# Token choice and experts in one stage, gathers twelve ahead, ranks summed into one result, closing layer norm in groups of four and three

## The chip, the core and the metric

The kernel runs on one core of a Trainium2 chip. Its engines work from queues of their own and wait for one another by semaphores: TensorE (PE) multiplies matrices into PSUM banks, VectorE (DVE) and ScalarE (ACT) read those banks, GpSimd (POOL) computes and issues the indirect DMAs (gathers of rows by a list of numbers), and SyncE (SP) issues the plain DMAs. The metric is the device time of one execution in microseconds.

## The reference

The input is x, 4 batches of 1024 tokens of width 256. Two layers follow, each an attention and a mixture of experts. The part that the change touches is the end of the second layer: the attention's closing layer norm with gamma and beta, the residual, and then the last mixture, cut here to its core.

```python
# attention of layer 1, its end; x is the residual before it
out = (out - mu) * rsqrt(var + LN_EPS) * gamma + beta          # out = ctx @ wo + bo + layernorm(x)
x = x + out
# mixture of layer 1, on xn = layernorm(x): B = 4, N = 1024, D = 256, E = 8 experts, M = N // E = 128
gate_logits = einsum('bnd,de->bne', xn, gate_w)
gates = sinkhorn(gate_logits)                                   # 8 iterations
vals, idx = top_k(swapaxes(gates, -1, -2), M)                   # each expert takes its 128 best tokens
routed = xn[b_idx, routed_indices]                              # gather of rows
outputs = einsum('ebmd,edf->ebmf', routed, experts) * gate_values
routed_back = zeros_like(xn).at[b_idx, routed_indices].set(outputs)   # a token in several experts keeps one
x = x + routed_back
```

## The kernel before, in words

x stays in on-chip memory as 32 tiles of 128 tokens. The program is a row of stages; `phase` opens each with a barrier, clears its semaphores and sets them (the ISA rows of line 73), four engines taking a quarter each. Inside a stage each engine's instructions stand in the order in which the code writes them; no scheduler moves them. The stages of which the change speaks:

`group_attention`: 512 units of scores. VectorE finds row maxima (L1986), ScalarE takes exponentials (L2029), PE multiplies (L2076, L2089, L2106). Behind the last unit VectorE makes the new x of tiles 0 to 27 in seven groups of four (`new_x`: L1966 scales, L1971 adds the kept x; GpSimd adds beta, L1957; `new_statistics`, L1977, takes the moments). `NEW_AT` says at which steps of the unit count VectorE does so; the steps lie between its waits for PE's context (L1996, L1998) and projection (L2004).

`gated_tiles`: eight groups of four tiles. VectorE normalises (`normalise`, L2204, tile gt_xn, two buffers), SP stores the rows for the gathers (routed_rows, L2192), PE turns them (L2279), ScalarE copies (L2243), PE makes the gate products (L2287), ScalarE copies (L2250), PE turns (L2295), ScalarE keeps the logits (L2254). The last four tiles get their closing norm here (`last_tiles`), and then ScalarE's second square root (L152) stands ahead of its copy of the second group.

`sinkhorn`: a chain between PE and VectorE, untouched.

`top_tokens`: PE turns the gates (L2412), VectorE takes for the 32 pairs of batch and expert their 128 best tokens, 8 at a time (L2432 to L2435), PE turns the list, VectorE writes m_index (L2442). Then 32 masks (L2446, one per pair, "which token is this", two buffers), each multiplied by PE in eight products of one column (L2421), and from the ranks the place of each token (L2449 to L2460).

`routed_experts`: SP loads the expert weights (L2488). GpSimd gathers the rows of pair n (L2509, four buffers, held until PE has turned pair n-4), PE turns (L2533), ScalarE copies (L2569), PE multiplies (L2544), VectorE scales by the gate (L2582, tile re_y, four buffers), SP stores (L2495, routed_outputs). Then GpSimd gathers for each of the 32 tiles its rows (L2519, re_got, four buffers, from the batch's results once all are stored), VectorE adds them to x (L2587), and SP stores the output (L2499), in a loop with a register count. All 64 gathers stand in one queue, and all 64 stores of results and output in another.

Of the kernel before, what the change touches and what calls it, by code (L numbers as in the profile page):

```python
# [1802 lines left out]
def group_attention(nc, g, parts, values, x_kept, qs, ks, v, gamma, beta, gw, gate):  # L1803
# [54 lines left out]
    with phase(nc) as (e, semaphore, begin):  # L1858
# [14 lines left out]
        NEW_AT = [UNITS + k for k in (3, 7, 14, 18, 22, 26, 30, 34)]  # L1873
# [291 lines left out]
def gated_tiles(nc, g, qs, gamma, beta, gw, logits, rows_out):  # L2165
# [4 lines left out]
    STEPS, TH = T // C, C // HALVES  # L2170
    with phase(nc) as (e, semaphore, begin):
        sb = lambda n, shape, dt=F32: e.enter_context(nc.sbuf_tensor(f"gt_{n}", shape, dt))
        sem = lambda n: semaphore(f"gt_{n}")
        xn = [sb(f"xn{u}", [P, C, D]) for u in range(2)]
# [6 lines left out]
        rows_kept = [sem(f"rows_kept{u}") for u in range(2)]  # L2181
# [5 lines left out]
        @block.sync  # L2187
        def _(sp):
            rows = rows_out.rearrange("(i c p) d -> i p c d", c=C, p=P)
            for i in range(STEPS):  # L2190
                sp.wait_ge(xn_ready, ONE + C * (i + 1))
                sp.dma_start(rows[i], xn[i % 2][:]).then_inc(rows_kept[i % 2], 16)  # L2192
            for u in range(2):
                sp.wait_ge(rows_kept[u], ONE + 16 * (STEPS // 2))

        @block.vector
        def _(dve):
            def normalise(i):
                if i >= 2:
                    dve.wait_ge(xnT_done, ONE + HALVES * (i - 1))  # L2200
                    dve.wait_ge(rows_kept[i % 2], ONE + 16 * (i // 2))
                for c in range(C):
                    t = C * i + c
                    nc.vector.tensor_scalar(xn[i % 2][:, c, :], g.x[:, t, :], g.mean[:, t:t + 1], g.rstd[:, t:t + 1],  # L2204
                                            ALU.subtract, ALU.mult).then_inc(xn_ready, 1)

            def last_tiles():
                tiles = range(READY, T)
                for t in tiles:
                    nc.vector.scalar_tensor_tensor(g.x[:, t, :], g.x[:, t, :], g.mean[:, t:t + 1], gamma[:],  # L2210
                                                   ALU.subtract, ALU.mult).then_inc(scaled_ready, 1)
                dve.wait_ge(scaled_ready, ONE + LATE_TILES)
                for t in tiles:
                    nc.vector.scalar_tensor_tensor(g.x[:, t, :], g.x[:, t, :], g.rstd[:, t:t + 1], kept_tiles(qs, t, 1)[:, 0],
                                                   ALU.mult, ALU.add).then_inc(x_ready, 1)
                dve.wait_ge(x_ready, ONE + LATE_TILES)
                nc.vector.tensor_tensor(g.x[:, READY:T, :], g.x[:, READY:T, :], beta[:].unsqueeze(1).broadcast_to([P, LATE_TILES, D]),
                                        ALU.add).then_inc(beta_ready, 1)
                dve.wait_ge(beta_ready, ONE + 1)
                for t in tiles:  # L2220
                    nc.vector.bn_stats(g.stats[:, t, :], g.x[:, t, :]).then_inc(stats_ready, 1)
                dve.wait_ge(stats_ready, ONE + LATE_TILES)
# [6 lines left out]
            last_tiles()  # L2229
            closing.moments(dve, 1, READY)  # L2230
            closing.inverses(dve, 1, READY)
            for i in range(2, STEPS):
# [407 lines left out]
```

## Time and profile before

| what | us |
|---|---|
| median of 3 runs (2344.79 to 2349.75) | 2348.84 |
| the profiled execution, its own time | 2363.76 |
| its span, first to last instruction | 2362.0 |
| attention's last stage ends, about | 2080 |
| first instruction of top tokens | 2152.7 |
| first gather of the experts | 2238.9 |

TensorE is busy 2011.9 us of the span (85%), VectorE 1704.1 (72%), ScalarE 1213.4 (51%), GpSimd 474.0 (20%). These are averages over stages with different limits: most of the span is attention and the first mixture, which the change does not touch. A row of the timeline gives the start, the duration, the engine, the line, the operation, what it writes and reads, how often, and in brackets how long the engine was idle before and what released it. "issue" means that it waited for nothing that the profile shows.

### The profile page before, as it was taken

The page shows a single profiled execution, that of the slowest core. Times are in us where ns is not written, and L with a number is a line of the kernel's source. Part 1 is how long each engine was busy: PE and PEld are TensorE (multiplying, and loading weights), DVE is VectorE, ACT ScalarE, POOL GpSimd, SP SyncE. Part 2 cuts the span into 40 slices and gives each one's busy share as a digit, 9 for nine tenths or more (in the row PEclk, how much of TensorE's full clock was granted, in tenths as well). Part 3 has the DMA queues.
Part 4 walks back from the last instruction along what each step waited for, and adds up shares of the span by engine and source line. Part 5 has one row for each costly group of instructions (what it writes and reads, how often), then busy time and mean ns, then how long its engine had stood idle before and what let it go on. Part 6 is the DMA issues. An engine that isn't in the chain of part 4 may idle for free. (4 is left out here: it accounts for less than half of the span.)

```text
span 2362.0 us, 49456 instructions
## 1 busy us (share of the span) xinstructions
PE 2011.9 (85%) x18325; PEld 1356.7 (57%) x18325; DVE 1704.1 (72%) x2695; ACT 1213.4 (51%) x2196; POOL 474.0 (20%) x610
## 2 busy tenths in 40 slices
PE   5889888799979999989978899999999999971270
PEld 4667666468879999978867333343343343330150
DVE  5666666566658888856644789999999999647822
ACT  4455454343256666632233278888888888530010
POOL 1010001010022322224343112112212211300054
PEclk9899999799989999999989589999999999675585
DMA  2000000191043333333268886854864701020054
GB/s 90 2 0 0 0 0 0 60 342 62 28 157 124 120 111 120 107 100 113 89 206 281 105 73 59 73 38 43 67 41 44 62 20 37 19 72 0 27 159 136
DMA packets 222809, 188.18 MB, mean 80 GB/s; under 512 B 121533, under 2 KB 201369, under 8 KB 220505
## 3 DMA queue, kind: packets, MB, share of 16 engines
q1 hardware_dynamic: 202872, 146.71, 30.9%
q0 software_dynamic: 18080, 27.17, 4.3%
q10 hardware_dynamic: 1728, 12.58, 1.5%
q8 instruction: 81, 1.33, 0.3%
q14 instruction: 48, 0.39, 0.1%
HBM read 121.37 MB, written 64.75 MB: 79 GB/s over the span
## 5 line engine op out<-in xcount | busy, mean ns | idle before, releaser
L2029 ACT ACTIVATE ga_probT<-banks 128x512 f32<-128x512 f32 x1024 | 556.7, 597 | 172.7 <-PE banks L2089 124.7
L1986 DVE TENSOR_REDUCE ga_nmax<-banks 128x1 fp32r<-128x1024 f32 x512 | 610.4, 1218 | 27.9 <-PE banks L2076 26.7
L2076 PE MATMUL banks<-a_ks,a_qs 48*128 48x512 f32 x1024 | 390.8, 465 | 9.5 <-PEq L77 5.7
L2089 PE MATMUL banks<-a_qs,a_ks 49*128 49x512 f32 x1024 | 390.1, 461 | 2.3 <-ACT ga_probT L2029 2.3
L2106 PE MATMUL banks<-ga_probT,a_v 128*32 128x256 f32 x4096 | 342.1, 408 | 6.2 <-ACT ga_o L2035 6.2
L2076 PEld LDWEIGHTS banks<-a_ks,a_qs 48*128 48x128 f32 x1024 | 158.9, 195 | 224.7 <-DVE ga_nmax L1986 171.5
L1952 POOL DMA_DIRECT2D a_qs<-ga_max_rows x256 | 130.8, 519 | 578.4 <-DVE ga_max_rows L1993 537.1
L1447 PE MATMUL banks<-rb_xT,rb_own_w 128*128 128x256 f32 x1872 | 232.1, 283 | 5.2 <-DVE rb_xT L1313 3.5
L1447 PEld LDWEIGHTS banks<-rb_xT,rb_own_w 128*128 128x128 f32 x1872 | 224.5, 190 | 11.5 <-issue 8.1
L2106 PEld LDWEIGHTS banks<-ga_probT,a_v 128*32 128x32 f32 x4096 | 82.9, 110 | 203.8 <-ACT ga_probT L2029 146.8
L1153 PE MATMUL banks<-m_xnT,sh_w 128*128 128x512 f32 x768 | 184.2, 398 | 6.6 <-DVE sh_w L942 5.3
L1289 POOL DMA_INDIRECT rb_xb<-normalised_rows,m_source x78 | 101.9, 1307 | 391.3 <-PE banks L1436 229.1
L2089 PEld LDWEIGHTS banks<-a_qs,a_ks 49*128 49x128 f32 x1024 | 158.1, 193 | 20.0 <-ACT ga_probT L2029 16.8
L1153 PEld LDWEIGHTS banks<-m_xnT,sh_w 128*128 128x128 f32 x768 | 145.9, 192 | 39.4 <-issue 9.5
L370 DVE TENSOR_REDUCE wa_nmax<-banks 128x4 f32<-128x512 f32 x128 | 87.0, 680 | 96.1 <-PE banks L584 96.1
L449 ACT ACTIVATE wa_probT<-banks 128x512 f32<-128x512 f32 x128 | 76.4, 597 | 136.3 <-PE banks L596 136.3
L1305 DVE TENSOR_TENSOR rb_own_w<-m_w,rb_own_w 128x1024 fp32r<-128x1024 f32 x78 | 95.2, 1221 | 68.7 <-ACT rb_own_w L1378 64.7
L1468 PE MATMUL banks<-rb_own_w,rb_glu 128*128 128x256 f32 x936 | 119.0, 283 | 3.4 <-DVE rb_own_w L1309 3.4
L1468 PEld LDWEIGHTS banks<-rb_own_w,rb_glu 128*128 128x128 f32 x936 | 112.1, 189 | 3.6 <-DVE rb_own_w L1309 3.6
L596 PE MATMUL banks<-ident,wa_prob 128*128 128x128 f32 x512 | 88.6, 298 | 23.5 <-ACT wa_prob L442 23.5
L442 ACT ACTIVATE wa_prob<-wa_ex 128x512 f32<-128x512 f32 x128 | 80.5, 629 | 52.2 <-DVE wa_ex L372 51.5
L278 POOL TENSOR_TENSOR wa_q_heads<-wa_q,wa_head_rows 128x512 f32<-128x512 f32 x32 | 32.6, 1039 | 365.9 <-ACT wa_q L483 365.9
(327 smaller groups left out, 3240.3 us busy)
## 6 DMA issues: line engine op xcount, KB each, us to landing
rb_w_f<-in_L_ffn_rw_dram SPq DMA_DIRECT2D x39, 512.0 KB
m_xnT<-xnT_parts ACTq DMA_DIRECT2D x12, 1024.0 KB, 4.8
sorted_out<-rb_yb SPq DMA_DIRECT2D x39, 256.0 KB, 2.1
m_w<-in_L_ffn_rw_dram SPq DMA_DIRECT2D x2, 4096.0 KB, 20.3
values<-pg_v SPq DMA_DIRECT2D x16, 512.0 KB, 3.1
a_v<-values SPq DMA_DIRECT2D x16, 512.0 KB, 8.8
a_qs<-queries_rounded SPq DMA_DIRECT2D x28, 256.0 KB, 8.6
a_ks<-keys_rounded SPq DMA_DIRECT2D x28, 256.0 KB, 10.4
```

Of the source, the lines that this page charges most:

```text
L596: last = nc.tensor.transpose(b_pt[k][:, P * j:P * (j + 1)], prob[k][:, j, :], g.ident[:])
L1153: last = nc.tensor.matmul(bank[m % 2][:], w[a][:, k, P * m:P * (m + 1)], xnT[s][:, b, k, :], start=(k == 0 and a + b == 0), stop=(k == KD ...
L1289: nc.gpsimd.indirect_dma_start(out=xb[j % 2][:, h, :], out_offset=None, in_=rows, in_offset=bass.IndirectOffsetOnAxis(ap=source[:, 2 * j + ...
L1305: nc.vector.tensor_tensor(flat(own_w[1]), of(w, n), flat(own_w[0]).bitcast(F32), ALU.subtract).then_inc(ready, 1)
L1447: last = nc.tensor.matmul(bank[h][:, R * m:R * (m + 1)], w[a][:, k, at:at + P], xT[b][:, k, :], start=(k == 0 and a + b == 0), stop=(k == ...
L1468: last = nc.tensor.matmul(b_y[:, D * r:D * (r + 1)], glu[a][:, m, P * r:P * (r + 1)], own_w3[b][:, m, :], start=(m == 0 and a + b == 0), s ...
L1952: nc.gpsimd.dma_start(dst, src).then_inc(max_in[1][b % 2], 16)
L1986: nc.vector.tensor_reduce(nmax[b % 2][:, at:at + 1], slot[:], axis=AX.X, op=ALU.max, negate=True).then_inc(use_read, 1)
L2029: nc.scalar.activation(probT[k % SETS][2 * h + n][:], b_t[ring_place["weights", w] % RING][:], ACT.Exp, scale=SCALE).then_inc(exp_ready, 1)
L2076: return nc.tensor.matmul(slot[:, HALF * kh:HALF * (kh + 1)], qs[a][rows, n, P * q:P * (q + 1)], ks[a][rows, n, HALF * kh:HALF * (kh + 1)] ...
L2089: nc.tensor.matmul(bank[:], ks[a][rows, 2 * gp + n, P * kt:P * (kt + 1)], qs[a][rows, 2 * gp + n, HALF * hf:HALF * (hf + 1)], start=True, ...
L2106: last = nc.tensor.matmul(b_o[at:at + BL, cols], v[c % SLOTS][:, h, 2 * gp + n, kt, :], probT[k % SETS][2 * h + n][:, cols], start=(kt == ...
```

## The change

It has three parts. First, `top_tokens` and `routed_experts` become one stage. The gathers start when the index is written; GpSimd may be twelve pairs ahead (`AHEAD`), with a buffer for each of the 32 pairs and of the 32 results; the masks stand between the scalings on VectorE, two beside each expert; the places are worked out at pair 16; the additions to x begin at pair 26. Second, each mask is multiplied by a matrix that is zero but for one column, so that all pairs add into one 32x1024 result, which is copied and turned once. Third, the closing layer norm: `NEW_AT` puts four groups ahead of VectorE's wait for the projection and three behind, and in `gated_tiles` three buffers let three more groups be normalised between the steps of the last four tiles.

```diff
-        NEW_AT = [UNITS + k for k in (3, 7, 14, 18, 22, 26, 30, 34)]
+        NEW_AT = [UNITS + k for k in (3, 4, 5, 6, 14, 15, 16, 17)]
...
-    STEPS, TH = T // C, C // HALVES
+    STEPS, TH, KEPT = T // C, C // HALVES, 3
...
             normalise(0)
             normalise(1)
-            last_tiles()
+            late_scaled()
+            late_sums()
+            normalise(2)
+            late_betas()
+            late_statistics()
+            normalise(3)
+            dve.wait_ge(stats_ready, ONE + LATE_TILES)
             closing.moments(dve, 1, READY)
+            normalise(4)
             closing.inverses(dve, 1, READY)
-            for i in range(2, STEPS):
+            for i in range(5, STEPS):
                 normalise(i)
...
+            pool.wait_ge(index_ready, ONE + 1)
+            for n in range(BE):
+                if n >= AHEAD:
+                    pool.wait_ge(t_done, ONE + n - AHEAD + 1)
+                if n >= SL:
+                    pool.wait_ge(taken_in[n % SL], 16 * (n // SL))
+                nc.gpsimd.indirect_dma_start(out=taken[n][:], out_offset=None, in_=rows,
+                                             in_offset=bass.IndirectOffsetOnAxis(ap=index[:, n:n + 1], axis=0)
+                                             ).then_inc(taken_in[n % SL], 16)
+            pool.wait_ge(zero_kept, ONE + 16 * B)
+            for t in range(T):
+                if t % TB == 0:
+                    for s in range(SL):
+                        pool.wait_ge(kept[s], ONE + 16 * (t // TB + 1) * (E // SL))
+                if t == 0:
+                    pool.wait_ge(place_ready, ONE + 1)
+                if t >= SL:
+                    pool.wait_ge(got_in[t % SL], 16 * (t // SL))
...
+            def ranks(n):
+                pe.wait_ge(is_ready, ONE + n + 1)
+                for h in range(2):
+                    cols = slice(S // 2 * h, S // 2 * (h + 1))
+                    last = nc.tensor.matmul(b_r[0:BE, cols], rank_col[:, BE - 1 - n:2 * BE - 1 - n], is_token[n % HOTS][:, cols],
+                                            start=(n == 0), stop=(n == BE - 1))
+                last.then_inc(rank_done, 1)
...
+            transposes(0)
             for n in range(BE):
+                if n + 1 < BE:
+                    transposes(n + 1)
+                products(n)
+                for m in range(LEAD + 2 * n, min(LEAD + 2 * n + 2, BE)):
+                    ranks(m)
+                if n == PLACES_AT:
+                    ranks_T()
...
+            for n in range(LEAD):
+                hot(n)
             for n in range(BE):
+                for m in range(LEAD + 2 * n, min(LEAD + 2 * n + 2, BE)):
+                    hot(m)
+                weighed(n)
+                if n == PLACES_AT - 1:
+                    dve.wait_ge(rank_done, ONE + BE)
+                    nc.vector.tensor_copy(ranks_s[:], b_r[0:BE, :]).then_inc(ranks_copied, 1)
+                if n == PLACES_AT:
+                    places()
+                if n >= ADDS_AT:
+                    added(n - ADDS_AT)
+            for t in range(BE - ADDS_AT, T):
+                added(t)
+
+
+LEAD, PLACES_AT, ADDS_AT, AHEAD = 2, 16, 26, 12
```

`transposes`, `products`, `weighed` and `added` are the steps of before, unrolled instead of looped by batch; `weighed` still has four buffers and waits for the store of pair n-4. SP's list is unchanged: the weights, the 32 stores of results, then the loop of 32 output stores.

On PE, where the masks and the experts meet (tt_ and re_ are the stages' prefixes; re_taken the gathered rows, re_w the weights, re_takenT the turned rows), the program before has:

```order
L2415 MATMUL banks<-ident,tt_top 128x32
L2416 MATMUL banks<-ident,tt_top_at_f 128x32
L2421 MATMUL banks<-tt_rank,tt_is_token 128x1 x256
L64 UNCONDITIONAL_BRANCH
L2523 UNCONDITIONAL_BRANCH
L2533 MATMUL banks<-ident,re_taken 128x128 x2
```

and the changed one, from the same two turns on:

```order
L2517 MATMUL banks<-ident,re_top 128x32
L2518 MATMUL banks<-ident,re_top_at_f 128x32
L2485 MATMUL banks<-re_is_token,re_rank_col 32x512 x4
L2501 MATMUL banks<-ident,re_taken 128x128 x4
L2509 MATMUL banks<-re_w,re_takenT 128x256 x2
```

The 256 one-column products ahead of the stage's end are gone; four products of 512 columns now stand behind each of the first 15 experts, and the next expert's turns stand between.

On VectorE in the gated tiles, around the last four tiles' norm, the difference is this (gt_xn is the normalised group, a_beta the added vector):

```order
 L142 RECIPROCAL rstd<-gt_std 128x32
 L2204 TENSOR_SCALAR gt_xn<-x,mean,rstd 128x256 x8
-L2210 SCALAR_TENSOR_TENSOR x<-x,mean,a_gamma 128x256 x4
-L2214 SCALAR_TENSOR_TENSOR x<-x,rstd,a_qs 128x256 x4
-L2217 TENSOR_TENSOR x<-x,a_beta 128x1024
-L2221 BN_STATS stats<-x 128x6 x4
+L2211 SCALAR_TENSOR_TENSOR x<-x,mean,a_gamma 128x256 x4
+L2217 SCALAR_TENSOR_TENSOR x<-x,rstd,a_qs 128x256 x4
+L2204 TENSOR_SCALAR gt_xn<-x,mean,rstd 128x256 x4
+L2222 TENSOR_TENSOR x<-x,a_beta 128x1024
+L2228 BN_STATS stats<-x 128x6 x4
+L2204 TENSOR_SCALAR gt_xn<-x,mean,rstd 128x256 x4
```

Eight normalisations now stand ahead of the second set of moments (L128 and following, behind this piece), which stood directly behind L2221.

## Rows read from the trace of the kernel before

**Rows 1.** Busy time by stretch: engine sums with instruction counts, clock, DMA share, GB/s.
```profile
2320.00:2340.00 20.00, 0.00 (x0) 0.00 (x0) 6.81 (x16) 0.00 (x0) 13.89 (x15) 0.50 0.42 124
```

**Rows 2.** Timeline of VectorE at the end of top tokens.
```profile
2217.63 0.19 DVE L2442 TENSOR_TENSOR m_index<-tt_indexT,tt_batch_row 128x32 uint32<-128x32 f32 x1
2217.74 15.27 DVE L2446 TENSOR_SCALAR tt_is_token<-tt_token,tt_indexT 128x1024 bf16<-128x1024 f16 x32
...
2236.35 0.18 DVE L2460 TENSOR_SCALAR m_place<-tt_row 128x32 uint32<-128x32 f32 x1
```

**Rows 3.** Timeline of GpSimd: first gather, first after the hole, last.
```profile
2238.93 1.04 POOL L2509 DMA_INDIRECT re_taken<-routed_rows,m_index  x1 [0.44 <-issue]
...
2303.44 0.94 POOL L2519 DMA_INDIRECT re_got<-routed_outputs,m_place  x1 [8.81 <-DVE x L2587]
...
2337.21 0.94 POOL L2519 DMA_INDIRECT re_got<-routed_outputs,m_place  x1 [0.30 <-DVE x L2587]
```

**Rows 4.** Tile re_taken: what ended engines' idle time, us and times.
```profile
  PE banks L2533: 13.9, 10
```

**Rows 5.** Timeline of SP: output stores, all, two single ones, the last 21.
```profile
2303.49 56.72 SPq L2499 DMA_DIRECT2D out_dram<-x  x32
...
2314.13 0.00 SPq L2499 DMA_DIRECT2D out_dram<-x  x1
...
2333.12 0.71 SPq L2499 DMA_DIRECT2D out_dram<-x  x1
...
2341.55 18.66 SPq L2499 DMA_DIRECT2D out_dram<-x  x21
```

**Rows 6.** DMA queues in 2324 to 2330: packets, MB, share. The only queue.
```profile
q0 software_dynamic: 240, 0.66, 37.0%
```

**Rows 7.** Timeline of PE in the experts; stretch 2254 to 2256, columns as rows 1.
```profile
2248.40 2.07 PE L2544 MATMUL banks<-re_w,re_takenT 128*128 128x256 f32 x4
...
2268.24 1.03 PE L2544 MATMUL banks<-re_w,re_takenT 128*128 128x256 f32 x4
2269.10 0.38 PE L2533 MATMUL banks<-ident,re_taken 128*128 128x128 f32 x2
...
2254.00:2256.00 2.00, 2.00 (x13) 1.74 (x12) 0.97 (x2) 0.77 (x2) 1.26 (x3) 1.00 0.60 187
```

**Rows 8.** Gated tiles: timeline of VectorE, ScalarE, PE; stretch 2100 to 2102.
```profile
2093.82 2.68 DVE L2204 TENSOR_SCALAR gt_xn<-x,mean,rstd 128x256 f32<-128x256 f32 x8
...
2093.20 0.30 ACT L152 ACTIVATE gt_std<-gt_var,gt_eps 128x4 f32<-128x4 f32 x1 [6.57 <-DVE gt_var L136]
2093.41 1.06 ACT L2243 ACTIVATE gt_xnT<-banks 128x512 f32<-128x512 f32 x2
...
2096.25 3.58 PE L2287 MATMUL banks<-gt_xnT,a_gw 128*8 128x512 f32 x4
...
2101.18 1.88 PE L2287 MATMUL banks<-gt_xnT,a_gw 128*8 128x512 f32 x4
...
2100.00:2102.00 2.00, 2.00 (x14) 1.17 (x14) 0.71 (x3) 1.62 (x4) 0.00 (x0) 1.00 0.68 234
```

**Rows 9.** Timeline around the entry into top tokens.
```profile
2151.00 0.42 DVE L2368 TENSOR_TENSOR m_gates<-sk_p,sk_expert_sum 128x256 f32<-128x256 f32 x1
2152.66 1.41 PEld L2412 LDWEIGHTS banks<-ident,m_gates 128*32 128x32 f32 x8 [4.56 <-issue]
```

**Rows 10.** Attention's end: timeline of VectorE; stretch 2040 to 2060.
```profile
2040.66 0.69 DVE L2004 TENSOR_TENSOR x<-banks,x 128x512 f32<-128x512 f32 x1 [11.93 <-PE banks L2134]
...
2042.05 1.66 DVE L1966 SCALAR_TENSOR_TENSOR x<-x,mean,a_gamma 128x256 f32<-128x256 f32 x4
...
2046.72 2.67 DVE L1966 SCALAR_TENSOR_TENSOR x<-x,mean,a_gamma 128x256 f32<-128x256 f32 x4
...
2052.40 2.68 DVE L1966 SCALAR_TENSOR_TENSOR x<-x,mean,a_gamma 128x256 f32<-128x256 f32 x4
...
2040.00:2060.00 20.00, 20.00 (x93) 6.30 (x91) 19.00 (x42) 10.37 (x19) 7.08 (x3) 0.50 0.00 1
```

More of the change, by code:

```diff
@@ L2369, in _, with routed_experts @@
                                         ALU.mult).then_inc(p_ready, 1)
-def top_tokens(nc, g, gates, index, value, place):
+def routed_experts(nc, g, gates, rows, outputs, out):
     E = gates.shape[3]
@@ new lines, in routed_experts @@
+        takenT = [sb(f"takenT{s}", [P, KD, M]) for s in range(SL)]
+        y = [sb(f"y{s}", [M, D]) for s in range(SL)]
+        got = [sb(f"got{t}", [P, D]) for t in range(T)]
+        zero = sb("zero", [1, D])
+        consts, gT_done, step, top_ready, topT_done, index_ready = [sem(n) for n in (
+            "consts", "gT_done", "step", "top_ready", "topT_done", "index_ready")]
+        is_ready, rank_done, place_ready = sem("is_ready"), sem("rank_done"), sem("place_ready")
+        ranks_copied, ranksT_done = sem("ranks_copied"), sem("ranksT_done")
@@ new lines, in transposes, with products @@
+            def transposes(n):
+                s = n % SL
+                pe.wait_ge(taken_in[s], 16 * (n // SL + 1))
+                if n >= TS:
+                    pe.wait_ge(t_ready, ONE + n - TS + 1)
+                for k in range(KD):
+                    last = nc.tensor.transpose(b_t[n % TS][:, M * k:M * (k + 1)], taken[n][:, P * k:P * (k + 1)], g.ident[:])
+                last.then_inc(t_done, 1)
+            def products(n):
+                pe.wait_ge(t_ready, ONE + n + 1)
+                if n >= YS:
+                    pe.wait_ge(y_ready, ONE + n - YS + 1)
+                for k in range(KD):
+                    last = nc.tensor.matmul(b_y[n % YS][:, 0:D], takenT[n % SL][:, k, :], w[:, n % E, k, :],
+                                            start=(k == 0), stop=(k == KD - 1))
+                last.then_inc(y_done, 1)
@@ L2597, in mixture1 @@
         gates = sb("gates", [P, TB, B, E])
-        index, value, place = sb("index", [M, BE], U32), sb("value", [M, BE]), sb("place", [P, T], U32)
         sinkhorn(nc, g, logits, gates)
-        top_tokens(nc, g, gates, index, value, place)
-        routed_experts(nc, g, rows, outputs, index, value, place, out)
+        routed_experts(nc, g, gates, rows, outputs, out)
 def program(nc, g, out):
```

277 lines of the change are left out of this document (108 added, 169 removed).

## The prediction

> **What bounds the kernel now.** I read the table by stretches first. Attention ends near 2080 us, gated tiles near 2119, Sinkhorn near 2151; then come top tokens to 2236.5 and routed experts to 2362.0. In the last two stages no compute engine is full: from 2320 to 2340 PE does nothing, VectorE works 6.8 us of 20, and even GpSimd, the busiest, 13.9 [rows 1]. So the end is set by a chain, not by a busy engine, and I followed it backwards in three timelines.
>
> VectorE has the experts' token numbers (m_index) at 2217.82 us. Then it makes 32 masks in 15.3 us and the places, done at 2236.53 [rows 2]. None of that is needed by the first gather, which yet starts at 2238.93 because it lies in the next stage [rows 3]. From there GpSimd issues 64 gathers, one each 1.25 us (0.95 busy, 0.30 between) when nothing holds it, the last ending at 2338.15: 99.2 us for a chain worth 64 x 1.25 = 80. The missing 19 us are holes: 13.9 us in ten waits for transposes that free one of four buffers, and one of 8.8 us [rows 3, 4] (3.3 of these 22.7 are the ordinary spacing).
>
> Last comes a tail of 23.85 us behind the last gather. In it SP issues 21 of the 32 output stores, 0.89 us each (18.66/21) [rows 5]. They are late though their rows were ready: while GpSimd gathers without a pause, SP's stores come ever farther apart: eight in the first 10.6 us (2303.49 to 2314.13), then four gaps of 6.9 us on average up to 2341.55, the last 8.4 [rows 5]. The queue view agrees: from 2324 to 2330 the queue that carries the stores moved nothing, while gathers filled 37% of the DMA engines [rows 6].
>
> **The change part by part.** The sum is made on the profiled execution (span 2362.0, own time 2363.76), then carried to the median 2348.84 by subtraction. The profiled one stands 0.6% above the median, which I carry over as it is.
>
> (a) *Start of the gathers.* They now wait for the index in the same stage: 2238.93 - 2217.82 = 21.1; with 0.1 for the wait, **-21.0**. The masks and places go beside the experts.
>
> (b) *The chain of 64 gathers.* Twelve ahead instead of four, and every result buffer separate. Ideal 79.9 (64 x 1.248) against 99.2: -19.3. What is late next: gather n needs the transposes of expert n-12, and PE now does two rank sums, four products in all, beside each of the first 15 experts. An expert costs 1.09 us at 2.4 GHz (2268.24 to 2269.10 the products, and 0.22 for the transposes), 2.5 at 1.2 GHz (2.07 + twice 0.22) [rows 7]. The new 32x512 product in bf16 has no row. From below it is the 256-column f32 pass, 0.26 us (1.03/4); from above the 512-column f32 pass, 0.47 (1.88/4) [rows 7, 8]. I take 0.26, since the operands are half as wide. So an expert with four such products is 1.09 + 1.04 = 2.13 at the high clock. I let PE begin at 2222, 4 us behind the first gather's issue, and I let it work 7 us at the low clock, as now from 2247 to 2254, when the granted clock is 1.00 [rows 7]: expert 15 at 2229 + 13.3 x 2.13 = 2257, the transposes of 19 at about 2262. Gather 31 would be ready to issue at 2218 + 31 x 1.25 = 2257. So **5 us** of stall come back (with 0.47 per product: 2229 + 13.3 x 2.97 + 4.4 = 2273, 16 us; with no price for the clock or products: 0). VectorE (two masks and one scaling, 3 x 0.48 = 1.4 us per expert) and the ring of four y buffers lie below 2.1. The copy of the ranks and the places (3.5 us now, from the masks' end at 2233.0 to 2236.53 [rows 2]; I count 5 for both) delay it at experts 15 and 16, covered by y banks three deep and gathers twelve ahead. Term: -19.3 + 5 = **-14.3**, ends -19 and 0.
>
> (c) *The tail.* Now one y store plus 11 output stores got out beside 28 gathers in 35 us. In the new order SP must first issue the last 12 to 15 y stores beside the 32 result gathers (40 us), and by the same rate that uses up what SP gets. So 29 to 32 output stores are left instead of 21: 8 x 0.89 = **+7**. From below: if SP keeps pace, 2 are left and the tail is 5, so -19; from above all 32 are left, +10. I take +7, by the rows in which SP and GpSimd work together.
>
> At this place the Trainium skill, "DMA: Bandwidth & Descriptors", section "Queues, rings and completion order", says otherwise: each DMA engine takes turns between its queues packet by packet. By it the stores would get their turns and the tail would be the lower end. The trace disagrees from 2314 on, with 6.9 us between stores, so the row decides and the rule is only a rival.
>
> (d) *Gated tiles.* On VectorE, eight normalisations (tiles 2 and 3 of four, 2.68 us) now stand ahead of the late moments [rows 8]. But ScalarE's square root still stands ahead of its second copy: now it waits 6.57 us for the moments and copies at 2093.41. It will copy at 2096.2. PE does the third transposes early, then stands idle until 2097.3, where now its gate products begin at 2096.25 [rows 8]: +1.05. PE has the low clock in them now (3.58 us for four, against 1.88 at the next step, when the granted clock is 1.00) [rows 8]; after a longer idle the rise moves from 2100 to some 2103, and 3 us of work at half speed cost up to 1.5 more. The steps behind are PE's own, 3.17 us each, so nothing gives it back. **+2.2**, ends 0 and +3.
>
> (e) *Stage entries.* One stage is gone (in (a)). The new one sets six semaphores per engine instead of two. The entry with two takes 1.24 us (2151.42 to 2152.66), that with three to four 1.66 (2236.53 to 2238.19) [rows 2, 9]; 0.28 each gives **+0.8** (0 to +1.2).
>
> (f) *Closing layer norm inside attention.* Four groups before VectorE's wait for the projection, three behind. A group takes 5.69 us; two more fit from 2028.7 to 2040.1, in an idle of 11.93 us that ends at 2040.66 [rows 10]. But PE is the bound there, 20.00 us busy in 20.00 at clock 0.50, and asks VectorE for nothing until the projection. **0** (if the groups overran by 3 us, 30 us of slack lie behind).
>
> (g) Ranks summed into one 32x1024 result, and turned: 256 small products leave, 64 and eight turns come. All of it is in (b).
>
> Sum: -21.0 - 14.3 + 7 + 2.2 + 0.8 = **-25.3**. 2363.76 - 25.3 = 2338.5 in the profiled state, 2348.84 - 25.3 = **2323.5** at the median.
>
> **The rivals.**
> 1. *SP keeps pace.* y stores now come beside gathers each 1.5 us without a queue; the starvation appears only after 10 us without a hole. With holes from PE the stores flow, output stores start near 2276 and follow the sums. Tail 5 instead of 31: -51, time 2298. Against it: the result gathers have no more holes than now.
> 2. *The port.* A mask is 0.477 us (15.27/32) for 1024 elements and now runs while GpSimd issues. In the rows an addition group of VectorE stretches from 1.67 to 2.67 us where GpSimd computes [rows 10]. If each mask holds up one gather for its length, 32 x 0.48 = 15.3 us enter the chain, less 5 already idle: +10, time 2334. The Trainium skill, "SBUF — State Buffer", section "Who interferes with whom", has this as a lock: VectorE's two-port modes block GpSimd wholly, descriptor writing included. No row of the present kernel has masks beside gathers.
> 3. *SP and GpSimd exclude each other.* 64 gathers x 1.25 plus 64 stores x 0.89 = 137 us from 2218, plus 2 at the end: 2357; with (d), (e) 2360, time 2347: no change.
> 4. *Slower: the y ring.* y stores pass four buffers. If, with GpSimd now never resting, each y store takes the 6.9 us that output stores take between 2314 and 2341, then 32 x 6.9 = 221 us stand in place of 44, and PE, then gathers, wait on it: 2218 + 221 + 31 + 3 = 2473, time 2460. The forecast has 32 experts in 44 us, 1.4 each, so it decides from 1.4 + 25.3/32 = 2.2 us per y store. For it: the spacing in [rows 5]. Against it: gathers stop when twelve ahead, and holes let stores through.
> 5. *Products nearly as dear as f32.* The upper end of (b), +11: 2334.
>
> **How the numbers follow.** Forecast and its own range (2310 to 2332): 0.48. Rival 1: 0.20. Rivals 2 and 5: 0.18. Rival 3: 0.06. Rival 4: 0.03, and milder forms of it that end between forecast and no change: 0.05. Within 0.2% (4.7 us, about what a measurement here can tell from no change) lies half of rival 3: 0.03. Slower: rival 4 and what rival 3 might overrun, 0.04. Faster: 0.93. Range 2297 to 2340: it takes rival 1 at its edge and leaves out rivals 3 and 4.
>
> **What would show it.** (a) First re_taken gather 0.1 to 0.3 us behind re_index. (b) 64 gathers within 80 to 88 us, holes only where transposes are late, between the 22nd and 32nd; the 32x512 products at 0.26 us when the clock is high. (c) From the last gather's end some 31 us with 29 or more output stores in it, and gaps of about 7 us between stores while GpSimd is full. (d) The second gt_xnT copy at about 3 us later after the stage's start. (f) PE as busy as now until the stage ends. The forecast falls if output stores follow the sums (rival 1), if a gather beside a mask takes over 1.3 us (rival 2), or if the scalings wait for their buffer most of the time (rival 4).

## The result, and the profile after

The changed kernel takes 2330.12 us (median of six runs, 2322.77 to 2333.79), the kernel before 2349.3 beside it. The ratio is 0.9912, with a 95% interval of 0.9887 to 0.9937: 19 us less, where 25 were forecast. Two later comparisons with the kernel unchanged gave 0.9958 (0.9925 to 0.9991) and 0.9916 (0.9886 to 0.9946). The time lies inside the range. But two of the large terms are wrong, and their errors partly cancel: it is inside by luck.

The two profiled executions differ by 41 us (spans 2362.0 and 2321.0), more than the medians. Most of the surplus lies ahead of the change's main part. The experts' token numbers (re_index, formerly m_index) are ready 22.6 us earlier, and that moment varies much between profiles of the same code: 2217.6 and 2202.2 us in two of the kernel before, 2195.1, 2195.8 and 2209.1 in three of the kernel after. So I compare from the start of that instruction to the span's end, "index to end" below: 144.4 and 141.0 us before, 125.9, 129.7 and 127.7 after. That is 15 us less on the means.

First the steps that came as forecast. VectorE's timeline at the index, then GpSimd's with the first gather right behind it (the answer to [rows 2, 3]):

```profile
2195.07 0.19 DVE L2560 TENSOR_TENSOR re_index<-re_indexT,re_batch_row 128x32 uint32<-128x32 f32 x1
```
```profile
2195.55 1.04 POOL L2463 DMA_INDIRECT re_taken<-routed_rows,re_index  x1 [63.75 <-DVE re_index L2560]
```

The wait is gone: 0.3 us from the index's end to the gather instead of 21.1. PE's timeline then shows the new rank products, which had no row before, beside an expert's own work (transposes, products):

```profile
2206.93 1.04 PE L2485 MATMUL banks<-re_is_token,re_rank_col 128*32 128x512 bf16 x4
2207.90 0.44 PE L2501 MATMUL banks<-ident,re_taken 128*128 128x128 f32 x2
2208.18 1.03 PE L2509 MATMUL banks<-re_w,re_takenT 128*128 128x256 f32 x4
```

Four 32x512 products take 1.04 us, 0.26 each, the lower end of the price, as chosen. From 2219.5 to 2244 an expert comes every 2.20 us (forecast 2.13), with PE busy 24.09 us of 24.50.

Now what came otherwise. Busy time by stretch (columns as in [rows 1]):

```profile
2196.00:2206.00 10.00, 8.65 (x29) 3.98 (x28) 3.40 (x9) 1.15 (x3) 7.57 (x9) 0.65 0.37 105
2206.00:2219.50 13.50, 8.18 (x32) 3.59 (x30) 2.79 (x7) 0.79 (x3) 8.65 (x9) 0.77 0.43 127
2219.50:2244.00 24.50, 24.09 (x101) 12.49 (x102) 13.32 (x31) 4.09 (x12) 10.39 (x11) 0.92 0.37 111
2251.00:2257.00 6.00, 6.00 (x34) 5.16 (x34) 2.36 (x6) 1.77 (x5) 4.72 (x5) 1.00 0.77 226
2257.00:2280.00 23.00, 6.88 (x22) 4.45 (x20) 2.60 (x6) 1.15 (x3) 17.24 (x19) 0.59 0.47 133
2280.00:2292.00 12.00, 5.99 (x14) 4.16 (x14) 5.46 (x16) 1.04 (x3) 0.79 (x2) 0.64 0.24 77
2292.00:2306.00 14.00, 0.00 (x0) 0.00 (x0) 6.21 (x18) 0.00 (x0) 11.53 (x8) 0.50 0.68 200
```

Between 2257 and 2280 PE, VectorE and ScalarE are all nearly idle (6.88, 2.60 and 1.15 us of 23), and GpSimd issues 19 gathers, about the most it can. Experts 26 to 31, which need 1.09 us each, take 34 us. This is ScalarE's timeline there, the copy of one expert's turned rows; "remote" is a wait whose end comes so late that the profile matches it to no instruction or transfer:

```profile
2255.40 0.38 ACT L2540 ACTIVATE re_takenT<-banks 128x256 f32<-128x256 f32 x1 [0.70 <-issue]
2258.85 0.38 ACT L2540 ACTIVATE re_takenT<-banks 128x256 f32<-128x256 f32 x1 [3.07 <-PE banks L2501]
2263.13 0.38 ACT L2540 ACTIVATE re_takenT<-banks 128x256 f32<-128x256 f32 x1 [3.90 <-remote]
2268.78 0.38 ACT L2540 ACTIVATE re_takenT<-banks 128x256 f32<-128x256 f32 x1 [5.26 <-remote]
2282.06 0.38 ACT L2540 ACTIVATE re_takenT<-banks 128x256 f32<-128x256 f32 x1 [12.90 <-remote]
```

The copy at 2282.06 belongs to the thirtieth expert and waits for PE alone, for that expert's two transposes. PE's timeline has them here:

```profile
2265.44 0.64 PE L2501 MATMUL banks<-ident,re_taken 128*128 128x128 f32 x2
```

They end at 2266.07, 16.0 us before the copy starts. The trace also records when PE's update of the semaphore took effect: 2282.04, and ScalarE starts 0.02 us later. So it is the producer's signal that is late, not the waiting engine. VectorE's scaling in the same stretch shows 9.69 us "remote". The experts' late rows then reach GpSimd:

```profile
2279.79 0.95 POOL L2475 DMA_INDIRECT re_got<-routed_outputs,re_place  x1 [0.30 <-issue]
2291.95 4.62 POOL L2475 DMA_INDIRECT re_got<-routed_outputs,re_place  x1 [11.21 <-DMA routed_outputs<-re_y]
2296.87 0.94 POOL L2475 DMA_INDIRECT re_got<-routed_outputs,re_place  x1 [0.30 <-issue]
```

A second standstill of this kind lies early, under the first gathers. The chain of waits from the index to the end, its five longest pieces:

```profile
2211.05 8.40 another core or an unknown queue
2258.87 4.24 another core or an unknown queue
2263.16 5.60 another core or an unknown queue
2268.80 13.24 another core or an unknown queue
2291.95 4.62 POOL re_got L2475
```

So the chain from the first gather to the end of the last became longer, 110.1 us instead of 99.2 (forecast 84.9). The tail behind it became shorter, 15.3 instead of 23.85 (forecast 31): GpSimd's hole of 11.2 us let the last y stores and two output stores out. In contrast to [rows 5], SP's timeline has all 32 output stores at 0.91 us apiece, 15 of them behind the last gather:

```profile
2290.14 29.12 SPq L2443 DMA_DIRECT2D out_dram<-x  x32
```

### The profile page after: what moved, and what is told of

Same layout as the page of the kernel before. It is cut to its first block and busy times, and to the rows that moved or that the text cites. A ratio compares the mean times of both kernels' runs of the same rounds, so it can differ in the third digit from the quotient of the medians.

```text
span 2321.0 us, 48875 instructions
## 1 busy us (share of the span) xinstructions
PE 1999.7 (86%) x18141; PEld 1345.6 (58%) x18141; DVE 1701.1 (73%) x2696; ACT 1214.0 (52%) x2196; POOL 480.5 (21%) x612
## 5 line engine op out<-in xcount | busy, mean ns | idle before, releaser
L2089 PE MATMUL banks<-a_qs,a_ks 49*128 49x512 f32 x1024 | 379.7, 451 | 2.3 <-ACT ga_probT L2029 2.3
L2106 PE MATMUL banks<-ga_probT,a_v 128*32 128x256 f32 x4096 | 331.0, 396 | 6.4 <-ACT ga_o L2035 6.4
L1447 PEld LDWEIGHTS banks<-rb_xT,rb_own_w 128*128 128x128 f32 x1872 | 224.7, 190 | 10.9 <-issue 7.6
L2089 PEld LDWEIGHTS banks<-a_qs,a_ks 49*128 49x128 f32 x1024 | 153.8, 188 | 15.5 <-ACT ga_probT L2029 12.4
```

The source lines that it names most:

```text
L1447: last = nc.tensor.matmul(bank[h][:, R * m:R * (m + 1)], w[a][:, k, at:at + P], xT[b][:, k, :], start=(k == 0 and a + b == 0), stop=(k == ...
L2089: nc.tensor.matmul(bank[:], ks[a][rows, 2 * gp + n, P * kt:P * (kt + 1)], qs[a][rows, 2 * gp + n, HALF * hf:HALF * (hf + 1)], start=True, ...
L2106: last = nc.tensor.matmul(b_o[at:at + BL, cols], v[c % SLOTS][:, h, 2 * gp + n, kt, :], probT[k % SETS][2 * h + n][:, cols], start=(kt == ...
```

## The experiments

The runs fell on three chips: e1 to e4 on the first, e5 to e8 on the second, e9 to e12 on the third. Which one gave the result above is not on record.

Two theories fit this profile, and two more had to be asked. Theory 1: while GpSimd issues indirect gathers one right behind another, the other engines' waits for each other end late. Theory 2: straight-line code is fetched late (the two loops over batches are unrolled now). Theory 3: the ring of four y buffers. Theory 4: PE's pace. Against theory 2 the trace already says that the instruction queues moved nothing between 2246 and 2310.

**Only the closing layer norm and the gated tiles, on the kernel before.**

```diff
-        NEW_AT = [UNITS + k for k in (3, 7, 14, 18, 22, 26, 30, 34)]
+        NEW_AT = [UNITS + k for k in (3, 4, 5, 6, 14, 15, 16, 17)]
 ... (gated_tiles as in the kernel after, top_tokens and routed_experts as before)
```

> Only the part on the closing layer norm and on the gated tiles (NEW_AT, the third xn buffer, the later tiles' work in pieces between the tiles) on the kernel before; choice of tokens and experts stay as they were. In the two profiled executions the last attention tiles (2000 to 2060 us) ran at a granted clock of 0.50 to 0.54 before and 0.71 to 0.82 after, and the index was ready 22 us earlier. If that is the work of this part: about 2330 us (ratio 0.99), and the granted clock of 2000 to 2060 is above 0.7 here too. If it is chance of the execution: 2350 to 2353 us (ratio 1.000 to 1.002), with +0.7 us from the gated tiles, and then the whole gain of 19 us comes from the merged stage.

Ratio 0.997 (0.9935 to 1.0005), index to end 142.0 us, the granted clock was 1.00 in 2000 to 2020 and 0.59 in 2020 to 2040. The clock there follows the execution, not the code: in the same two stretches a second profile of the kernel before had 0.74 and 0.83, one of the kernel after 1.00 and 0.60. Whether this part gives nothing or up to 15 us isn't settled by so wide an interval. The rest of the gain is put down to the merged stage.

**Experts' gathers four ahead.**

```diff
-LEAD, PLACES_AT, ADDS_AT, AHEAD = 2, 16, 26, 12
+LEAD, PLACES_AT, ADDS_AT, AHEAD = 2, 16, 26, 4
```

> The kernel after with the experts' gathers four ahead instead of twelve. Theory 1 (a run of indirect gathers that GpSimd issues one right behind another holds up the other engines' waits, on ScalarE and VectorE above all): GpSimd pauses from the fifth gather on, the 8.4 us of standstill at 2211 to 2219.5 go or shrink to 2 us, the first result gather starts 6 to 8 us earlier, and the time is 2321 to 2325 us (after: 2330); the standstills under the result gathers stay. Theory 2 (straight-line code that is fetched late) and theory 3 (the ring of four y buffers): the standstill stays where it is, 2329 to 2332 us. Theory 4 (PE's pace, twelve ahead is needed to feed it): every gather's landing, 2.7 us, now shows in part, 2335 us or more.

0.9903 (0.9875 to 0.9931), index to end 128.8 us: no faster than after, so as a time my expectation missed. But the profile says more. The 8.4 us standstill is gone, also the one among experts 26 to 31 nearly (last y store issued at 2267.4 instead of 2289.4), and the 32 result gathers have no hole: GpSimd's group of them is

```profile
L2475 POOL DMA_INDIRECT re_got<-routed_outputs,re_place x32 | 30.4, 950 | 9.7 <-issue 9.7
```

in 39.8 us, 2258.3 to 2298.1. The chain is then 98.4 us, 11.7 less than after, and all of it comes back in the tail: five output stores got out beside the gathers, at distances up to 8.4 us, and 27 were left, 30.0 us of tail against 15.3.

```profile
2281.25 0.70 SPq L2443 DMA_DIRECT2D out_dram<-x  x1
...
2289.65 0.70 SPq L2443 DMA_DIRECT2D out_dram<-x  x1
...
2298.05 0.70 SPq L2443 DMA_DIRECT2D out_dram<-x  x1
...
2303.64 22.74 SPq L2443 DMA_DIRECT2D out_dram<-x  x27
```

**Result gathers behind the last expert.**

```diff
-                        pool.wait_ge(kept[s], ONE + 16 * (t // TB + 1) * (E // SL))
+                        pool.wait_ge(kept[s], ONE + 16 * B * (E // SL))
-LEAD, PLACES_AT, ADDS_AT, AHEAD = 2, 16, 26, 12
+LEAD, PLACES_AT, ADDS_AT, AHEAD = 2, 16, 32, 12
```

> The kernel after with the result gathers held back until all 32 experts' rows are kept, and the additions behind the last expert. Theory 1: with no gather beside them experts 23 to 31 run at 1.09 us each as experts 17 to 22 did, the last y store is issued at about 2262 and the 32 gathers run from about 2264 to 2304; behind them some 20 output stores of 0.88 us are left, so the end is at about 2323 of the span (now 2321), 2330 to 2334 us. Theories 2 and 3: the last nine experts take 34 us as now (2255 to 2289) and the gathers end at 2330, 2350 us or more.

0.994 (0.9905 to 0.9974), 2343 us; index to end 137.8. Theory 1's mechanism is borne out: without gathers beside them the last eleven copies of ScalarE come 1.08 to 1.29 us apart and nothing is "remote".

```profile
2262.35 0.38 ACT L2540 ACTIVATE re_takenT<-banks 128x256 f32<-128x256 f32 x1 [0.70 <-PE banks L2501]
...
2273.40 0.38 ACT L2540 ACTIVATE re_takenT<-banks 128x256 f32<-128x256 f32 x1 [0.70 <-PE banks L2501]
```

The time missed by 10 us. The early standstill was longer here (two y stores were 9.95 us apart), so the gathers began at 2278, 74.6 us behind the index instead of 69, and the tail was 23.2 us instead of 19.

**Eight y buffers.**

```diff
-    y = [sb(f"y{s}", [M, D]) for s in range(SL)]        # and kept likewise
+    y = [sb(f"y{s}", [M, D]) for s in range(8)]
```

> The kernel after with eight y buffers and eight kept semaphores instead of four. Theory 3 (the experts stand still since a y buffer is not stored yet): the holes before the multiplications by value go, experts end at 2262 instead of 2289, the hole of 11.2 us in the result gathers goes, 2316 to 2320 us. Theories 1 and 2: nothing is moved by it, 2329 to 2332 us, holes on VectorE and ScalarE at the same places.

0.9928 (0.9894 to 0.9962), index to end 129.0: theory 3 falls. ScalarE's timeline has the same row of standstills:

```profile
2266.21 0.38 ACT L2540 ACTIVATE re_takenT<-banks 128x256 f32<-128x256 f32 x1 [4.59 <-remote]
2271.89 0.38 ACT L2540 ACTIVATE re_takenT<-banks 128x256 f32<-128x256 f32 x1 [5.29 <-remote]
2284.53 0.38 ACT L2540 ACTIVATE re_takenT<-banks 128x256 f32<-128x256 f32 x1 [12.26 <-remote]
```

**A pause at every fourth, and at every eighth result gather** (both with four ahead).

```diff
+                if t and t % 4 == 0:          # 8 in e6_pause8 and e11_pause8_again
+                    pool.wait_ge(got_in[(t - 1) % SL], 16 * ((t - 1) // SL + 1))
```

> The kernel after with the experts' gathers four ahead (as in e2_ahead4) and a pause in the result gathers: every fourth waits until the one before it has landed, some 1.7 us. In e2_ahead4's profile the 32 result gathers ran without a gap (2258.3 to 2298.1), SP issued only 5 of 32 output stores beside them, at distances of 5.7 to 8.4 us, and the 27 others behind them, 27.9 us. Theory 1 (a run of back-to-back gathers holds up engines that wait for another engine): the stores flow at 0.9 to 1.5 us in and after each pause, the gathers take 40 + 7 x 1.7 = 52 us, 3 to 6 stores are left, 5 us: index to end 59 + 52 + 6 = 117 us (e2: 128.8, after: 125.9), the time 2319 to 2323. If the stores lag for another reason (the DMA engines' turns, as the prediction had it): they stay behind, 40 + 12 + 25, 2340 us.

> As e5_pause4 with the pause at every eighth result gather. Theory 1: within each run of eight (10 us) the distance of the stores grows to 5 or 7 us, and a pause of 1.7 us lets 1 or 2 through; gathers 40 + 3 x 1.7 = 45 us, some 18 stores left, 18 us: index to end 59 + 45 + 18 = 122 us, the time 2324 to 2328. If what counts is the number of pauses and not the length of a run, 24 stores are left and 2331.

Index to end is 121.1 us with seven pauses and 111.8 with three. A pause adds 2.5 to 3.4 us, where I had counted 1.7. In both the stores follow the gathers: two and three are left behind the last, where I had expected 18 with the pause at every eighth. These two profiles can't say that the pauses did it, since on this chip long runs held nobody up either (below). In the profiles of the two other chips the start of the hold-up can be dated: the first step that takes over 4.5 us begins 10.5 to 11.4 us after the run of gathers did (kernel after: 2195.55 and 2206.17, 2196.26 and 2206.71, 2209.60 and 2220.82; eight y buffers: 2199.51 and 2210.14; results last: 2204.07 and 2215.50; before: 2303.44 and 2314.13, [rows 5]; in its second profile after 13.5). That is eight or nine gathers in. It holds for runs behind a quiet stretch. Where other gathers had ended only 1.3 to 1.4 us earlier, such a step came sooner: 6.5 us into the run of eight in the kernel before (2284.93 and 2291.41), 5.1 us in e1_norm_alone (2274.68 and 2279.75), 7.3 us in e11_pause8_again (2254.69 and 2261.97).

The times of these two were odd, though. On that chip the kernel before took 2326 us, and the ratios were 1.001 (0.9972 to 1.0048) and 0.9967 (0.9949 to 0.9984), with 2319 to 2323 and 2324 to 2328 us expected against a kernel before of 2357.

**Plain loads in place of the result gathers.**

```diff
-                nc.gpsimd.indirect_dma_start(out=got[t][:], out_offset=None, in_=outputs[t // TB], ...
+                nc.gpsimd.dma_start(got[t][:], outputs[t // TB][P * (t % TB):P * (t % TB + 1), :]) ...
```

> As e2_ahead4 with the 32 result gathers replaced by plain loads of 128 rows in their order on GpSimd's queue (the rows are not put back in their tokens' places, so the output differs). It asks what in a run holds the others up. If it is the making of 128 descriptors from indices: the plain loads are issued faster or slower, and SP's stores flow beside them at 0.9 to 1.5 us each, with fewer than 8 stores left behind them. If it is the traffic of GpSimd's queue as such: the same distances of 5 to 8 us and over 20 stores left.

Index to end 93.4 us, five stores left. But the loads came mostly in twos to fours with waits of 0.8 to 1.8 us between, so there never was a long run, and the chip is the one where long runs of gathers held nobody up: it doesn't tell indices from traffic.

**The same pause in the kernel before.**

> The kernel before with the pause of e5_pause4 in its result gathers and nothing else. In its profile 21 of 32 output stores were left behind the last gather, 21.7 us, and the stores beside the gathers came at distances of 3.6 to 8.4 us. Theory 1: the gathers take 12 us more (part of it in the wait of 9.8 us that is there), the stores left shrink from 21 to 3 to 6: -15 to -17 us; the sum is -5 to -3 us, 0.998 of before. The other cause (the DMA engines' turns): +12 us, 1.005.

Index to end 130.7 us, 10 to 14 less than in both profiles of the kernel before, and three stores left instead of 21 and 19, as theory 1 has it. Yet the time was 1.0083 (1.0036 to 1.0129) of the kernel before on this chip, the wrong way. The profile says why the comparison misleads. Up to the fourth result gather its code is the kernel before's, and there, with 28 gathers from 2250.76 to 2284.72 and never over 0.51 us between two, ScalarE's copies are never more than 2.4 us apart and keep their pace to the end of the run:

```profile
2250.76 0.94 POOL L2509 DMA_INDIRECT re_taken<-routed_rows,m_index  x1 [0.51 <-PE banks L2535]
...
2284.72 0.95 POOL L2521 DMA_INDIRECT re_got<-routed_outputs,m_place  x1 [0.30 <-issue]
```
```profile
2281.41 0.38 ACT L2571 ACTIVATE re_takenT<-banks 128x256 f32<-128x256 f32 x1 [0.70 <-PE banks L2535]
2282.59 0.38 ACT L2571 ACTIVATE re_takenT<-banks 128x256 f32<-128x256 f32 x1 [0.79 <-PE banks L2535]
2283.67 0.38 ACT L2571 ACTIVATE re_takenT<-banks 128x256 f32<-128x256 f32 x1 [0.70 <-PE banks L2535]
```

So no hold-up is there for a pause to take away. Two runs of the kernels unchanged followed:

> The kernel before, unchanged, for a second profile. The runs e5 to e8 were on another chip than e1 to e4: there the kernel before took 2326 us instead of 2357, a pause in its result gathers made it 17 us slower instead of faster, and in e6_pause8's profile SP's output stores came at 1.2 us beside runs of eight gathers, where e2_ahead4's profile on the first chip had 5.7 to 8.4 us. Theory 1a (runs of back-to-back gathers hold the other engines up on some chips or in some executions only): each profile shows the one or the other. Where the hold-up is missing, output stores follow the gathers at 1.25 us, 2 to 4 are left behind the last gather instead of 21, and index to end is 118 to 124 us; where it is there, 142 to 146 as in the two profiles so far. Theory 1b (the hold-up comes from the profiler's own traffic and the chips differ in something else): this profile has it on any chip.

> The kernel after, unchanged, on the same chip as e9_before_again. Without the hold-up the merged stage does what its order allows: first result gather 53 us behind the index (now 56), 32 gathers in 40 us, end 3 us later: index to end 95 to 100 us, 20 to 25 us less than the kernel before there, ratio 0.989 to 0.991. With the hold-up: 124 to 127 us against 142 to 146, ratio 0.991 to 0.992.

They fell on the third chip (before 2353.5 us there). The hold-up was in both: output stores 5.65, 7.70 and 7.72 us apart and 19 left in the one, in the other copies of ScalarE 8.1, 9.9 and 11.3 us apart; index to end 141.0 and 129.7, ratio 0.9958 (0.9925 to 0.9991). Last, the pause and the kernel after side by side:

> e6_pause8 unchanged, beside the kernels before and after on one chip. In eight profiles the standstills begin some 10 to 11 us after the start of a run of back-to-back gathers (8 or 9 gathers in), and grow to 8.4 us a step; runs of at most eight stay under that. If that is the rule on this chip too: the stores come at 1.2 us beside the gathers, at most 4 are left behind the last one, index to end 110 to 114 us against 125 to 130 (after) and 141 to 145 (before): 0.985 to 0.988 of before and 0.994 of after. If it goes as on the chip of e5 to e8, where the times were 0.997 of before: 0.995 to 1.000 of before, and the profile of after (e12_after_third) should then show no standstill, with an index to end of 95 to 100 us.

> The kernel after, unchanged, on the same chip as e11_pause8_again. With the standstills (as in two profiles so far): the first at 10 to 11 us behind the first gather, experts' end and the result gathers' hole of 11 to 15 us, index to end 125 to 130 us, 0.991 to 0.996 of before. Without them: 95 to 100 us, 0.98 to 0.99 of before, and faster than e11_pause8_again by about 9 us, the price of its three pauses.

The pause at every eighth gave 0.9856 (0.9804 to 0.9907) of the kernel before, the kernel after 0.9916 beside it: 2319.3 against 2335.5 us. So this version beats both kernels on this chip. It differs from the kernel after by four ahead too, which alone changed nothing that could be measured on the first chip. Index to end is 114.1 against 127.7, with six stores left against 16. GpSimd's timeline shows one run of eight and the pause behind it, and SP's shows twelve stores around that run, eight of them beside it, 1.2 us apart where the run without pauses had 8.4:

```profile
2286.72 0.95 POOL L2477 DMA_INDIRECT re_got<-routed_outputs,re_place  x1 [3.40 <-DMA re_got<-routed_outputs,re_place]
...
2295.48 0.94 POOL L2477 DMA_INDIRECT re_got<-routed_outputs,re_place  x1 [0.30 <-issue]
2299.70 0.94 POOL L2477 DMA_INDIRECT re_got<-routed_outputs,re_place  x1 [3.27 <-DMA re_got<-routed_outputs,re_place]
```
```profile
2285.04 13.65 SPq L2443 DMA_DIRECT2D out_dram<-x  x12
```

One gap of 8.5 us is left in it, between y stores: right ahead of the first eight result gathers stand five of the experts' without a hole, a run of thirteen from 2254.69. ScalarE stands still in it:

```profile
2258.45 0.39 ACT L2542 ACTIVATE re_takenT<-banks 128x256 f32<-128x256 f32 x1 [0.70 <-issue]
2261.97 0.38 ACT L2542 ACTIVATE re_takenT<-banks 128x256 f32<-128x256 f32 x1 [3.14 <-PE banks L2503]
2266.97 0.39 ACT L2542 ACTIVATE re_takenT<-banks 128x256 f32<-128x256 f32 x1 [4.62 <-remote]
2273.33 0.38 ACT L2542 ACTIVATE re_takenT<-banks 128x256 f32<-128x256 f32 x1 [5.97 <-remote]
```

The same code on the second chip, in e6_pause8, did not stand still there, though its run was longer: eighteen gathers from 2238.15 to 2259.59 (GpSimd's timeline), and 13 to 15 us into it ScalarE keeps its pace:

```profile
2238.15 1.10 POOL L2463 DMA_INDIRECT re_taken<-routed_rows,re_index  x1 [1.41 <-PE banks L2503]
...
2259.59 0.95 POOL L2477 DMA_INDIRECT re_got<-routed_outputs,re_place  x1 [0.30 <-issue]
```
```profile
2251.07 0.38 ACT L2542 ACTIVATE re_takenT<-banks 128x256 f32<-128x256 f32 x1 [0.70 <-PE banks L2503]
2252.16 0.38 ACT L2542 ACTIVATE re_takenT<-banks 128x256 f32<-128x256 f32 x1 [0.70 <-PE banks L2503]
2253.43 0.38 ACT L2542 ACTIVATE re_takenT<-banks 128x256 f32<-128x256 f32 x1 [0.89 <-PE banks L2503]
```

## Why the prediction was right or wrong

**(a) Start of the gathers: right.** Forecast -21.0, measured -20.8: 0.3 us behind the index where 21.1 stood.

**(b) The chain: wrong in sign.** Forecast -14.3, measured +10.9. PE's part was right: 2.20 us for an expert with ranks, 0.26 for a product. The early standstill taken off, the 31 gathers behind the first take 53.7 - 8.4 = 45 us, where the forecast had 44. The step that failed is the list of what comes late next. I named PE, VectorE and the y ring, each with its work, and none of them is late through its work. I had seen that gathers without a hole keep SP's stores back [rows 5], and priced it for SP alone. In these profiles it holds for what waits on PE as well, and filling the holes with gathers twelve ahead makes the long runs that set it off: with four ahead the early standstill went, with the result gathers held back the late one. In the kernel before the experts' gathers waited ten times for a free buffer [rows 4], and I booked these waits as 13.9 us lost; between them only the last run, of eight, held a step up, by 5.0 us (ScalarE, 2291.4 to 2296.4). That those holes let the other engines run fits these profiles. On the second chip the same code ran nearly without them, and nobody stood still.

**(c) The tail: right as a mechanism, wrong in its case.** Forecast +7, measured -8.5. The forecast supposed result gathers without a hole. Four ahead makes just that case, and there the tail is 30.0 us with 27 stores, against 31 and 29. In the kernel after the standstill of the experts opened a hole of 11.2 us. The prediction set the spacing of the stores against the rule of turns between queues in the Trainium skill, "DMA: Bandwidth & Descriptors", section "Queues, rings and completion order". That reading does not hold: already SP's issues are that far apart. One turn of SP's loop is six instructions in the trace, the store and five of register work and branching, which the timeline leaves out. In the kernel before they take 0.03 to 0.37 us each around 2304. From 2325 to 2341 nearly all take 0.70 us or more, most of them 0.70 apart, though only one of the six waits for another engine. In e2_ahead4 it is the same from 2281 on, and twelve such steps are the 8.4 us. A store's first packet comes 4.4 to 7.0 us behind its issue there, and what holds it back until then isn't shown; all its packets are then done within 1.0 us beside the gathers. So these runs neither refute the rule nor bear it out.

(b) and (c) together: forecast -7.3, measured +2.4. The time came inside the range because the error of (b), 25.2 us, was met by one of (c), 15.5 us the other way; nothing in the prediction foresaw that.

**(d), (e): right within 1.5 us.** The gated tiles take 39.14 us instead of 38.45, +0.7 (forecast +2.2). The moments are waited for 8.91 us instead of 6.57, and PE's gate products begin later, as foretold, at the same 3.58 us; the clock's rise was not put off:

```profile
2071.63 0.30 ACT L152 ACTIVATE gt_std<-gt_var,gt_eps 128x4 f32<-128x4 f32 x1 [8.91 <-DVE gt_var L136]
```
```profile
2072.95 3.58 PE L2300 MATMUL banks<-gt_xnT,a_gw 128*8 128x512 f32 x4 [5.54 <-ACT gt_xnT L2256]
```

The entry into the merged stage takes 1.99 us instead of 1.24, +0.75 (forecast +0.8; four more semaphores at the prediction's own 0.28 each would have made 1.1).

**(f): open.** Forecast 0; the run of this part with (d) alone gave -7 us, with an interval from -15 to +1.

**The sum.** (a) to (c) take away 18.4 us in the two profiles and 15 on the means of all that were taken, and (d) and (e) give back 1.4 ahead of the index; the medians say 19.2, 11.6 and 18.8 less. Forecast 25.3.

**The rivals.** Rival 1 (SP keeps pace where there are holes) is true of the mechanism and happened in part: the tail came by a hole. Its time needed holes without their cost. Rival 2, the port: the masks ran beside gathers only at a few places. Here two of them cover one gather, which takes 0.97 us:

```profile
2208.56 0.88 DVE L2565 TENSOR_SCALAR re_is_token<-re_token,re_indexT 128x1024 bf16<-128x1024 f16 x2
```
```profile
2208.58 0.97 POOL L2463 DMA_INDIRECT re_taken<-routed_rows,re_index  x1 [0.30 <-issue]
```

The same is seen at 2213.6 (0.97) and, for most of a gather, at 2219.7 (0.94); the longest gather that touches a mask took 1.16. A lock for the length of a mask would add up to 0.48 for each one. The Trainium skill, "SBUF — State Buffer", section "Who interferes with whom", states such a lock; these rows do not show it. Rival 3 fails by the eight stores beside one run of eight gathers, 9.7 us in all, where one after the other they would need 17. Rival 4, the y ring: y stores were up to 10.5 us apart, as it said, but eight buffers changed nothing. The rows are made late, not stored late. Rival 5: the product is 0.26.

**What stays open.** First, why a run of gathers holds the others up. It strikes PE's signals, for which ScalarE and VectorE wait (recorded up to 16.0 us after PE's work ended in the kernel after, up to 18.2 in its second profile), and SP's own instructions; VectorE's waits for landed gathers end on time (additions every 1.25 us in the kernel before from 2304 to 2338).

Theory 1b, that recording the execution takes part in it, was not tested, and the record speaks for it in one form. Each gather's landing counts as 16 updates in the kernel's waits, so 64 gathers should leave 1024 records of them in the trace. The profiles of e5, e6 and e7 have all 1024, that of e8 1023, and in none of the four does a long run of gathers hold anyone up. All the others miss more than half (the kernel before has 250, the kernel after 395, e11_pause8_again 463), and all of them have the hold-up. SP's register instructions that take 0.70 us while waiting for nobody fit this as well. Every timed execution on record was recorded in this way, so no run tells what an unrecorded one does. As stated in the expectation, that recording causes it on any chip, the theory is wrong.

Second, what is different on the second chip. If the part ahead of the index took there what it took in any profile (2194 to 2229 us), the kernel before, at 2326, leaves 97 to 132 us for the rest, less than its 141 to 144 elsewhere. With the runs of 18 and 28 above, which held nobody up, this speaks for a hold-up that is missing on that chip, where a pause then only costs. For the experts of the kernel before e8_before_pause4 shows it; for its result gathers and for the kernel after it isn't shown, since neither was profiled there unchanged, nor was the changed kernel timed there. What the change is worth without the hold-up is open. Third, part (f).

## What to carry to other kernels

A wait that looks like loss can be what lets the others through: before filling an engine's holes, ask who used them. Where GpSimd issues more than about eight indirect gathers in a row, look at the other engines' waits 10 us into the run, and try one short wait every eight; here it was worth 16 us on one chip, together with four ahead, and in the kernel before a pause at every fourth cost 0.8% on another. So time it on more than one. When an engine's own register instructions slow down too, and records are missing, suspect the recording as well. Compare from a marker behind the noise (here the index) when profiles of the same code differ by more than the change.

## What the runs showed of the hardware

- Beside back-to-back indirect gathers (128 rows of 1 KB, one each 1.25 us) steps of the other engines came late, in most runs behind a quiet stretch from 10.5 to 11.4 us into the run (once 13.5); the distance of their steps grew to 8.4 us and more, and fell back when GpSimd paused for 3 us. Seen in the profiles of the result and on two chips; on another, whose profiles miss no landing records, runs of 18 and 28 gathers did not do it.
- In the kernel after, between 2258 and 2285, PE's semaphore updates are recorded up to 16.0 us after the work they stand for, and ScalarE starts 0.02 us behind the update. SP's loop instructions took 0.70 us each, 0.70 apart, instead of 0.03 to 0.37 (kernel before, 2325 to 2341).
- Beside a run of eight gathers SP's 128 KB stores kept 1.2 us apart. A pause of 1.4 us between runs does not wipe out what went before: the thirteen gathers above held ScalarE up from the sixth on.
- PE falls to the clock of 1.2 GHz in such a standstill (granted clock 0.50 from 2262 to 2282, after PE had been busy 2.88 us of 6; products 2.08 us instead of 1.03), which adds to it.
- The first result gather behind the long hole was followed by the next only 4.92 us later in all three profiles of the kernel after (4.93 with eight y buffers), against 1.25 elsewhere. Why, no run asked.
